# Softmax denominators of two head pairs in one pass of four 32-column tiles, numerators of the first pair parked in SBUF

## The reference

```python
q = (x @ Wq.T).reshape(b, t, 8, 64)
kv_latent = x @ Wkv_down.T                     # rank 64
k = (kv_latent @ Wk_up.T).reshape(b, t, 8, 64)
v = (kv_latent @ Wv_up.T).reshape(b, t, 8, 64)
attn = softmax(einsum('bqhd,bkhd->bhqk', q, k) * 64 ** -0.5, axis=-1)
out = einsum('bhqk,bkhd->bqhd', attn, v).reshape(b, t, 512) @ Wo.T
```

## Time and profile before

| | before |
|---|---|
| median of 3 runs | 1350.66 us (1349.06 to 1352.53) |
| the profiled execution | 1348.0 us, of it 1346.3 us span |
| PE busy | 1154.9 us, 86% |
| DVE busy | 991.3 us, 74% |
| POOL busy | 947.7 us, 70% |
| ACT busy | 745.6 us, 55% |
| denominators on PE (line 1186) | 252 records, 64.8 us busy |

### The profile page before, as it was taken

One profiled execution on the slowest core, in us unless ns is written; L12 is line 12 of the kernel. 1 busy time (PEld: TensorE's weight loads), 2 busy tenths in 40 slices (PEclk: granted clock), 3 DMA queues, 4 the chain that ended last, 5 costly groups with the idle time before them and its releaser, 6 DMA issues. The chain is left out here.

```text
span 1346.3 us, 23671 instructions
## 1 busy us (share of the span) xinstructions
PE 1154.9 (86%) x5973; PEld 774.5 (58%) x5974; DVE 991.3 (74%) x2224; ACT 745.6 (55%) x1448; POOL 947.7 (70%) x1086
## 2 busy tenths in 40 slices
PE   7899999999999999999999999999983166989400
PEld 6456566666656566666656566666642145989400
DVE  4888687777768677777777687767675885777596
ACT  4665667656665667656665667566532511444254
POOL 4686978788796978788786978787673205545268
PEclk9999999999999999999999999999995556999755
DMA  4000101010110101010110101010114303232474
GB/s 153 17 19 17 48 17 64 1 64 16 47 47 16 48 16 63 0 63 16 47 48 16 47 16 48 2 49 1 48 48 130 74 1 94 48 94 47 104 247 164
DMA packets 68478, 70.91 MB, mean 53 GB/s; under 512 B 12912, under 2 KB 64032, under 8 KB 68272
## 3 DMA queue, kind: packets, MB, share of 16 engines
q1 hardware_dynamic: 46800, 47.18, 10.9%
q10 hardware_dynamic: 16896, 16.78, 3.7%
q0 software_dynamic: 4704, 6.11, 2.9%
HBM read 40.35 MB, written 29.45 MB: 52 GB/s over the span
## 5 line engine op out<-in xcount | busy, mean ns | idle before, releaser
L705 ACT ACTIVATE PF<-PS 128x512 f32<-128x512 f32 x512 | 298.3, 595 | 256.5 <-PE PS L1087 248.3
L979 DVE TENSOR_REDUCE NMAX<-PS 128x1 f32<-128x512 f32 x512 | 342.6, 681 | 87.6 <-PE PS L1096 84.0
L567 POOL TENSOR_TENSOR SF<-SF,PF 128x512 f32<-128x512 f32 x252 | 322.9, 1303 | 14.0 <-ACT PF L705 13.9
L1168 PE MATMUL PS<-PF,V 128*64 128x512 f32 x1024 | 248.0, 605 | 0.0
L1086 PE MATMUL PS<-Q,K 128*128 128x512 f32 x512 | 221.4, 432 | 3.2 <-ACT PF L705 3.2
L1096 PE MATMUL PS<-K,Q 128*128 128x512 f32 x512 | 205.5, 402 | 10.5 <-DVE NMAX L979 10.2
L1087 PE MATMUL PS<-Q,K 128*128 128x512 f32 x512 | 201.3, 393 | 0.0
L724 ACT ACTIVATE Q<-PS 64x512 fp32r<-64x512 f32 x256 | 151.5, 592 | 47.9 <-PE PS L172 42.9
L644 POOL TENSOR_TENSOR XL<-XF,XH 128x512 fp32r<-128x512 f32 x63 | 83.1, 1319 | 128.2 <-ACT XH L779 128.2
L1086 PEld LDWEIGHTS PS<-Q,K 128*128 128x128 f32 x512 | 96.1, 188 | 120.3 <-issue 55.2
L564 POOL TENSOR_TENSOR SF<-PF 128x512 f32<-128x512 f32 x126 | 162.4, 1304 | 3.6 <-ACT PF L705 3.1
(11 more groups left out here) (351 smaller groups left out, 2490.2 us busy)
## 6 DMA issues: line engine op xcount, KB each, us to landing
X<-in_L_attn_x SPq DMA_DIRECT2D x16, 512.0 KB, 3.4
MODB<-mod_rows SPq DMA_DIRECT2D x16, 512.0 KB, 3.7
h_rows<-H ACTq DMA_DIRECT2D x16, 512.0 KB, 3.0
acc_rows<-H ACTq DMA_DIRECT2D x16, 512.0 KB, 4.1
out_x<-X SPq DMA_DIRECT2D x16, 512.0 KB, 2.9
A<-acc_rows SPq DMA_DIRECT2D x15, 512.0 KB, 8.7
W1F<-in_L_ffn_W SPq DMA_DIRECT2D x3, 1024.0 KB, 5.0
W2F<-in_L_ffn_W SPq DMA_DIRECT2D x3, 1024.0 KB, 6.6
```

The lines of the kernel that those rows point to most:

```text
L567: s_sum.done(pool.tensor_tensor(total, total, tile, ALU.add))
L705: s_exp.done(act.activation(PF[:, u % 8, :], st_bank(u), ACT.Exp))
L979: s_mred.done(dve.tensor_reduce(NMAX[:, p % 2, r:r + 1], mx_bank(u), AX.X, ALU.max, negate=True))
L1168: last = pe.matmul(num_bank(p)[odd * R:(odd + 1) * R, :], V1[:, vp, c, :], PF[:, k % 8, :], start=(c == 0), stop=(c == TC - 1))
```

## The change

The four denominator jobs of a batch become two. Job g covers the pairs 2g and 2g + 1: four matmuls of 32 output columns each, one for each head, fill the 128 partitions of a bank. They run in slots 20 and 36, ahead of the PV matmuls of the slot and behind its small jobs. Since the PSUM bank of the even pair's numerators is needed again before that, ACT copies those numerators into a new SBUF tile NUMS in slots 10 and 26. DVE then does one transpose for the group, eight reciprocals of 32 x 16, and for each pair a transpose back and a multiplication, spread over four slots instead of three; the even pair is multiplied in place in NUMS, the odd pair goes into XF as before. XH and XL move from slots 16, 24, 32, 40 (41 for the last XL) to 23, 25, 38, 40 and one later. In the last batch the second group stays as two single pairs, in the old form. POOL's first sum of pairs 0 and 2 now waits for the denominator job of the group before.

```diff
-    AHEAD, PV_AT, ADD_LAG, DIV_AT, XH_AT, NORM_AT, MOD_AT, OUT_AT = 13, 4, 2, 12, 16, 19, 41, 63
+    AHEAD, PV_AT, ADD_LAG, NORM_AT, MOD_AT, OUT_AT = 13, 4, 2, 19, 41, 63
+    XH_AT, FINAL_XH, FINAL_DEN, KEEP_AT = (23, 25, 38, 40), (23, 25, 32, 40), {2: 28, 3: 36}, (10, 26)
-    AT = {..., ("den", 0): 12, ("den", 1): 20, ("den", 2): 28, ("den", 3): 36, ...
+    AT = {..., ("den", 0): 20, ("den", 1): 36, ...
...
 # POOL
                 if c == 1:
-                    s_den.wait(pool, b, p - 2)
+                    s_den.wait(pool, b, p // 2 - 1)
...
-                    if n % 8 == (XH_AT + 1) % 8:
+                    for p, xb in outputs_due(b, n, 1):
...
-                            s_xlo.done(pool.tensor_tensor(XL[:, p, :], XF[:, :], XH[:, p, :].bitcast(F32), ALU.subtract))
+                            s_xlo.done(pool.tensor_tensor(XL[:, p, :], outputs(p, xb)[:, :], XH[:, p, :].bitcast(F32), ALU.subtract))
...
 # ACT
+                    for g, tb in due(KEEP_AT, b, n):
+                        if not (final(tb) and g):
+                            s_pv.wait(act, tb, 2 * TC * g + TC - 1)
+                            s_xlo.wait(act, tb - 1 + g, 2 - 2 * g)
+                            s_kept.done(act.activation(NUMS[:, :], num_bank(2 * g), ACT.Copy))
...
-                    if n % 8 == XH_AT % 8:
+                    for p, xb in outputs_due(b, n, 0):
+                        s_x.wait(act, xb, normalised(xb, p))
...
 # DVE, for group g: parts 0 to 3 stand in slots AT["den", g] + part
+                if (part, place) == (0, 1):
+                    s_den.wait(dve, xb, g)
+                    s_x.done(dve.transpose(XF[:, :], job_bank(DENS[g])))
+                elif (part, place) == (1, 0):
+                    for i in range(2):
+                        for k in range(4):
+                            head = slice((2 * i + k // 2) * 32, (2 * i + k // 2 + 1) * 32)
+                            s_x.done(dve.reciprocal(RDEN[k * 32:(k + 1) * 32, i, :], denominators(XF[head, :])))
+                elif (part, place) in ((1, 1), (2, 1)):
+                    s_x.done(back(XF[:, :], RDEN[:, part - 1, :]))
+                elif (part, place) == (2, 0):
+                    s_kept.wait(dve, xb, g)
+                    s_x.done(dve.tensor_tensor(NUMS[:, :], NUMS[:, :], XF[:, :], ALU.mult))
+                elif (part, place) == (3, 0):
+                    s_x.done(dve.tensor_tensor(XF[:, :], num_bank(1), XF[:, :], ALU.mult))
...
 # PE, now ahead of the PV matmuls
+                    for job in JOBS.get(n, []):
+                        kind, g, off = job
+                        if kind == "den" and exists(b + off) and not (final(b + off) and g):
+                            wait_job_bank(pe, b, job)
+                            s_sum.wait(pe, b + off, 4 * (TC - 1) * (g + 1) - 1)
+                            for head in range(4):
+                                last = pe.matmul(job_bank(job)[head * 32:(head + 1) * 32, :], ONE[:, 0:32], SF[:, head // 2, head % 2, :],
+                                                 start=True, stop=True)
+                            s_den.done(last)
```

More of the change, by code:

```diff
@@ L387, in attention, with normalised, outputs, outputs_due @@
     FREED = {"mrow": (s_mrow, 1, 0), "proj": (s_y, 1, 0), "q": (s_qlo, 2, 1), "n1t": (s_nf, 1, 0), "lat": (s_klo, 1, 0),
-             "vt": (s_v, 1, 0), "h2t": (s_h2c, 1, 0), "lg": (s_lgc, 1, 0), "den": (s_x, 4, 0)}
+             "vt": (s_v, 1, 0), "h2t": (s_h2c, 1, 0), "lg": (s_lgc, 1, 0), "den": (s_x, GROUP_OPS, 0)}
     DENS = {job[1]: job for job in ORDER if job[0] == "den"}
+    def normalised(b, p):
+        if final(b) and p >= 2:
+            return GROUP_OPS + 4 * (p - 2) + 3
+        return GROUP_OPS * (p // 2) + TIMES[p % 2]
+    def outputs(p, b):
+        return XF if p % 2 or final(b) and p == 2 else NUMS
+    def outputs_due(b, n, lag):
+        found = []
+        for p in range(H // 2):
+            for at, last in ((XH_AT[p] + lag, False), (FINAL_XH[p] + lag, True)):
+                xb = b - at // UNITS
+                if at % UNITS == n and exists(xb) and final(xb) == last:
+                    found.append((p, xb))
+        return found
     def at_slot(job):
@@ L418, in wait_job_bank @@
                 return
-            if banks[kind, idx, off] == banks[job] and exists(bb):
+            if banks[kind, idx, off] == banks[job] and exists(bb) and not (kind == "den" and idx and final(bb)):
                 stream, each, last = FREED[kind]
@@ L800, in norm_stats, with back @@
                         st.done(dve.bn_aggr(MV[:, k, :], NS6[:, k, :]))
[L802 to L808, removed]
-                if (part, place) == (0, 1):
-                    s_den.wait(dve, xb, p)
+            def back(dst, reciprocals):
+                return dve.transpose(dst, reciprocals.unsqueeze(2).broadcast_to([P, T // 32, 32]))
@@ L811, in normalise, with normalise_pair @@
+            def normalise_pair(xb, p, part, place):
+                base = GROUP_OPS + 4 * (p - 2)
+                if (part, place) == (0, 1):
+                    s_den.wait(dve, xb, p - 1)
                     s_xhi.wait(dve, xb, p - 1)
                     s_xlo.wait(dve, xb, p - 1)
-                    den = final_den if final(xb) and p == H // 2 - 1 else job_bank(DENS[p])
-                    s_x.done(dve.transpose(XF[:, :], den))
+                    s_x.done(dve.transpose(XF[:, :], final_den[p - 2]))
@@ L821, in normalise @@
+                    s_x.done(back(XF[:, :], RDEN[:, 0, :]))
                 elif (part, place) == (2, 0):
-                    s_x.wait(dve, xb, 4 * p + 2)
+                    s_x.wait(dve, xb, base + 2)
                     s_pv.wait(dve, xb, TC * p + TC - 1)
                     s_x.done(dve.tensor_tensor(XF[:, :], num_bank(p), XF[:, :], ALU.mult))
+            def normalise(b, n, place):
+                for part in range(4):
+                    for g in range(2):
+                        at = AT["den", g] + part
+                        xb = b - at // UNITS
+                        if at % UNITS == n and exists(xb) and not (final(xb) and g):
+                            normalise_group(xb, g, part, place)
+                    for p, start_at in FINAL_DEN.items():
+                        at = start_at + part
+                        if at % UNITS == n and final(b - at // UNITS):
+                            normalise_pair(b - at // UNITS, p, part, place)
@@ L1179, in body @@
                                     s_den.done(last)
[L1180 to L1188, removed]
+                    if final(b) and n == FINAL_DEN[2]:
+                        s_mred.wait(pe, b, UNITS - 1)
+                        for odd in range(2):
+                            s_sum.wait(pe, b, 2 * (TC - 1) * 3 - 2 + odd)
+                            last = pe.matmul(final_den[0][odd * R:(odd + 1) * R, :], ONE[:, :], SF[:, 0, odd, :], start=True, stop=True)
+                        s_den.done(last)
             batches(pe, body)
```

56 lines of the change are left out of this document (32 added, 24 removed).

## The result

The changed kernel takes 1463.45 us (median of 4 runs, 1459.92 to 1468.05) against 1351.53 for the kernel before on the same chip: a ratio of 1.0828 [1.0812, 1.0845], 112 us or 8.3% slower. The forecast was 1454 us in a range of 1424 to 1480. The profiled execution is 1459.92 us with a span of 1457.9.

The account below looks back on a forecast made before the run. PE was taken to set the pace; the terms sum to +6.9 us a batch, +103.8 over 15 transitions, and -0.7 in the last batch. On 1348.0 profiled that gives 1451, with 2.7 for the median 1454 us, range 1424 to 1480.

Parts of the forecast that it names:

- Slot 4: PE's denominators in bank 6 wait for ACT's row copy, +0.65, plus 0.14 for the job: +0.80 us a batch.
- slot 15: `q` 0, now behind `lat` in bank 6, waits for DVE's low keys: +1.40 us a batch.
- The remainders: Slots 6 to 10: XH behind ACT's `q` 3 copies delays POOL's XL of pair 3 and PE's first projection: +4.2 us.
- costed at nothing: DVE's eight reciprocals for one, 1.8 us more a job, taken as covered because DVE gets the sums 1.7 us earlier.
- The clock: PE's idle gap of 3.7 us ahead of the projection lowers the clock to half: +1.4 us a batch (0 to 3.4).
- The rival that it stays up: The clock does not fall in the attention: 1.4 x 15 less, 1433 us; chance 0.13.
- two slow stretches: Rival: PE's gap spans a stretch edge, giving two half-clock stretches a batch: 1.7 x 15 more, 1480 us; chance 0.06.
- Four tiles: Slots 20 and 4: the new denominator job's four 32-column tiles run in 1.00 us on PE, +0.14 each.
- the rival of two by two: The four denominator tiles run in two pairs: 0.86 us more for each of some 30 jobs, 1480 us; chance 0.10.
- Slots 20 to 26: XH of pair 0 between ACT's exponentials delays PE's scores, +0.25; NUMS multiplication with both inputs in SBUF, +0.45 us.
- The point at which it decides: Slot 10: whether XL of pair 3 lands no later than today relative to PE's transposes; 5.5 us shorter changes the sign.
- The rival "faster": POOL's wait is covered and PE's saved 1.43 us a batch come through: 1329 us; chance 0.04.

Follow-up runs that it names:

- edit 7: Changed kernel with only the `mrow` transpose moved from slot 4 to slot 3, away from the denominators: 1468.47 us.
- edit 2: Changed kernel with `proj` 1 pinned to bank 6 again, so that `lat` and `q` 0 use different banks: 1439.03 us.
- edit 3: Kernel before with only the new bank order (`proj` 1 in bank 7, `lat` in bank 6): 1377.98 us, ratio 1.0207.
- e4_busy_gap: Also written edit 5: changed kernel with 14 extra 512-column matmuls on PE ahead of the first projection's wait in slot 10: 1445.47 us.
- edit 1: Changed kernel with POOL forming XL of pair 2 two slots later, in slot 9 instead of 7: 1407.19 us.
- edit 10: Kernel of edit 9 with group 0's transposed reciprocals written to the denominators' PSUM bank, leaving the NUMS multiplication one SBUF input: 1364.43 us.
- edit 6: Changed kernel with the multiplication of NUMS replaced by a same-size transpose with one input, leaving out even pairs' numerators: 1464.52 us.
- edit 4: Changed kernel with the two four-tile denominator jobs moved back behind the PV matmuls of their slot: 1480.22 us.
- edit 8: Changed kernel with the 14 extra PE matmuls ahead of the first projection and the `mrow` transpose in slot 3: 1442.50 us.
- edit 9: Changed kernel with `proj` 1 pinned to bank 6, `mrow` in slot 3, and pair 2's XH in slot 7, XL in slot 9: 1373.75 us.

## Why the prediction was right

The mechanism and its order of sizes held: four new waits a batch on the engine that sets the pace, against 1.43 us of work saved. By the prediction's own terms:

- **Slot 4** (+0.80 predicted, +0.86 measured) and **slot 15** (+1.40, +1.40): each wait, its releaser and its length are in PE's list. Edits 7 and 2 took each away, and edit 3 put the second into the kernel before, with the same 1.39.
- **The remainders** (+4.2): 4.30 in slots 7 to 10 without the clock (`e4_busy_gap`: 0.64 + 3.66). The 0.64 in slots 7 and 8 is a wait for DVE, whose reciprocals were costed at nothing; it lies ahead of the wait for XL, which is the shorter for it, and it is still there, as +0.65 and +0.58, once that wait is mended (edits 1 and 10). The copies of `q` 3 hold up XH, XH holds up POOL, and four POOL jobs stand behind it: edit 1 moved only XL and took 4.0 us a batch, slow stretch included.
- **The clock** (+1.4): with the fall avoided a batch is 1.1 shorter on average over ten batches, of which two had no fall; those two take 66.4 and 66.6 us and their neighbours 67.7 to 68.1, so a fall costs about 1.5. The rival that it stays up is out, and so is that of two slow stretches in the changed kernel itself; edits 6 and 7 met the longer stretch that it described.
- **Four tiles** (1.00 a job): 1.00 to PV's start, so all four run together and the rival of two by two is out. By the 2.38 times that the Trainium skill (TensorE: Matmul & The Clock Gate, Part 3) gives for three column tiles, the prediction's estimate of the job was some 0.2 longer; the trace doesn't show that here. Slots 12, 28 and 20 gave -0.85 (at full clock), -0.87 and +0.14 where -0.86, -0.86 and +0.14 stood.
- **Slots 20 to 26** (+0.70): the term was too small; slots 23 to 27 cost 1.10. Edit 6 took 0.72 of it away: this is the second SBUF input, for which 0.45 stood. The multiplication of NUMS takes 1.26 us on average against the 0.69 of line 824 before. The other 0.38 stands where 0.25 was taken for XH. The eight reciprocals, costed at nothing, take 2.18 us; with the second input gone slot 23 is +0.09, so their cover holds as long as they stand ahead of PV, and edit 4 shows it gone.
- **The ends**: the 13 batches up to slot 4 of batch 14 were to cost 90 and cost 89.2. The distance to 1454 lies on both sides of them. Batch 0 has no projection of a batch before it, so up to slot 4 of batch 1 the prediction's terms give +0.5 (1.40 + 0.14 + 0.70 - 0.86 - 0.86); measured were 5.9, with the 4.3 ahead of the first bound. Behind slot 4 of batch 14 lie two more waits for XL, and the terms give some 12.6; measured were 16.5 (15.9 + 0.6). Slot 10 costs +5.15 in batch 14 and +5.02 in batch 15 (a wait of 4.20 us for XL at 1069.25, and a half-clock stretch of 6.83 us from 1066.98), and 2.9 lie behind the last bound. The causes of these 4 us were not tested.
- **The point at which it decides** was misjudged. The rival "faster" was tied to XL of pair 3 alone, with a change of sign beyond 5.5 us a batch. But by the prediction's own sum the chain's 4.2 and the clock's 1.4 leave +1.3 a batch when both are gone. Edit 1 ended at +3.07, and edit 10, with four waits mended, still at +0.32: all the terms together decide.

The mends show the sum from the other side: without the chain, the bank, the row copy and group 0's second SBUF input, the rest is 12.5 us (edit 10), and the kernel comes back to even only with its other jobs placed anew.

## What to carry to other kernels

Work taken from the busiest engine counts only after every in-order queue that the moved steps pass through has been followed. Here a copy moved behind four others on ACT held up POOL, and POOL held up PE three times as long as the change had saved. If banks or places are handed out by a loop, print its result for both kernels: here the two removed jobs moved two others together and cost about a fifth of the whole loss. And mend a wait that idles TensorE before the small ones: as long as it also lowers the clock, the small ones' gain may not be seen.

## What the runs showed of the hardware that was not expected

- A loop's period can settle on the rhythm of the clock's falls. In edits 6 and 7 some 0.6 us of waits a batch were removed, and the batch stayed at 68.2 to 68.3 us, because the half-clock stretch grew from 3.41 to 6.83 us. With PE's gap filled (edits 5 and 8), one of these removals gave its 0.68 us; with the gap mended (edits 9 and 10), the other gave 0.64 (+0.96 to +0.32). The lengths of the batches and of the stretches are measured; that one follows from the other was tested for edit 7, by edit 8, and is argued for edit 6.
- A reciprocal of 32 x 16 takes 245 ns, nearly the 254 of 128 x 16, and eight come at a pitch of 272 (2.18 us, edit 4): a quarter of the partitions costs the same.
- Engines can stand still with no wait in the profile, near the end of the batch loop: PE for 2.31 and 2.20 us in edits 5 and 8, followed by 3.41 and 6.83 us at half clock, and POOL for 4.2 to 4.9 us in batch 14 of the changed kernel and of edits 1, 9 and 10, where it costs up to 4 us. No run shows why.
